# First stage of a graph, attention and expert layer: tiles reordered, third x buffer, S product in plain fp32

## The reference

```
xn  = layernorm(x)
gnn: xt = xn @ weight (4 heads x 64); alpha_l, alpha_r = per-head dot products
     alpha = softmax over heads of leaky_relu(alpha_l[src] + alpha_r[dst])
     out[n] = sum over heads of alpha[n,h] * xt[dst[n], h]      (first 6250 edges only)
mix: qkv = xn @ w_qkv + b; k, v = layernorm per head (8 heads x 32)
     kv = einsum('nd,ne->de', k, v) / 6250 per head;  ret = q @ kv + xn
     out = gelu(ret @ w1 + b1) @ w2 + b2 + xn
x1  = x + gnn + mix
ffn: 8 experts, each relu(bn(. @ W1)), relu(bn(. @ W2)), @ Wo, softmax-weighted by a router
out = x1 + ffn(layernorm(x1))
```

## Time and profile before

| | us |
|---|---|
| median of 3 runs | 1238.53 (1236.17 to 1239.48) |
| the profiled execution | 1239.76 |
| its span, first to last instruction | 1237.8 |
| stage A, first matmul of tile 0 to that of tile 48 | 29.29 to 221.70 |
| between the stages | to 249.29 |
| busy: TensorE / VectorE / ScalarE / GpSimd | 1140.5 / 855.7 / 760.6 / 366.5 |

### The profile page before, as it was taken

One profiled execution on the slowest core, in us unless ns is written; L12 is line 12 of the kernel. 1 busy time (PEld: TensorE's weight loads), 2 busy tenths in 40 slices (PEclk: granted clock), 3 DMA queues, 4 the chain that ended last, 5 costly groups with the idle time before them and its releaser, 6 DMA issues. The chain is left out here.

```text
span 1237.8 us, 19690 instructions
## 1 busy us (share of the span) xinstructions
PE 1140.5 (92%) x6753; PEld 1007.6 (81%) x6753; DVE 855.7 (69%) x1861; ACT 760.6 (61%) x1289; POOL 366.5 (30%) x365
## 2 busy tenths in 40 slices
PE   1878789539999999999999999999999999999998
PEld 1666678438888988988889888888888888888887
DVE  7777678555758677586775967758677586765653
ACT  2667667216666666666666666666666666666665
POOL 2455543460605115051150511505014060220100
PEclk9999899768999999999999999999999999999999
DMA  3343331210001010010100101002010010000000
GB/s 110 104 113 112 95 90 53 74 35 1 19 1 48 6 35 18 1 48 5 36 18 1 48 6 35 19 1 53 1 35 18 5 49 1 21 5 15 4 1 22
DMA packets 60652, 42.16 MB, mean 34 GB/s; under 512 B 26248, under 2 KB 58732, under 8 KB 60552
## 3 DMA queue, kind: packets, MB, share of 16 engines
q1 hardware_dynamic: 56440, 34.28, 10.2%
q0 software_dynamic: 4112, 6.61, 2.2%
HBM read 27.87 MB, written 13.00 MB: 33 GB/s over the span
## 5 line engine op out<-in xcount | busy, mean ns | idle before, releaser
L1097 DVE SCALAR_TENSOR_TENSOR accumulated<-bank,router_w,accumulated 128x256 f32<-128x256 f32 (+1 forms) x392 | 169.9, 478 | 196.7 <-PE bank L220 163.1
L505 ACT ACTIVATE h<-weight_stage 128x512 fp32r<-128x512 f32 (+1 forms) x208 | 114.7, 599 | 209.1 <-PE bank L220 207.0
L218 PE MATMUL bank<-ffn_w_high,h 128*128 128x256 f32 (+1 forms) x784 | 221.8, 283 | 1.0 <-DVE h L901 1.0
L220 PE MATMUL bank<-ffn_w_high,h 128*128 128x256 f32 (+1 forms) x784 | 221.8, 283 | 0.0
L219 PE MATMUL bank<-ffn_w_low,h 128*128 128x256 f32 (+1 forms) x784 | 221.8, 283 | 0.0
L901 DVE TENSOR_TENSOR h_low<-activated,h_high 128x512 fp32r<-128x512 f32 (+1 forms) x208 | 154.6, 756 | 68.0 <-ACT h_high L505 68.0
L601 ACT ACTIVATE weight_stage<-bank,bn_cols 128x512 f32<-128x512 f32 (+1 forms) x208 | 156.8, 754 | 56.8 <-PE bank L220 56.5
L601 ACT ACTIVATE activated<-bank,bn_cols 128x512 f32<-128x512 f32 (+1 forms) x208 | 157.0, 755 | 54.1 <-PE bank L220 52.2
L476 POOL TENSOR_TENSOR residual<-residual,b_rows 128x1024 f32<-128x1024 f32 (+1 forms) x13 | 29.6, 2274 | 522.4 <-DVE residual L1116 522.4
L218 PE MATMUL bank<-xT_high,ffn_w_high 128*128 128x512 f32 (+1 forms) x416 | 163.2, 392 | 0.0
L220 PE MATMUL bank<-xT_high,ffn_w_low 128*128 128x512 f32 (+1 forms) x416 | 159.8, 384 | 0.0
(11 more groups left out here) (188 smaller groups left out, 2234.1 us busy)
## 6 DMA issues: line engine op xcount, KB each, us to landing
x_rows<-in_x SPq DMA_DIRECT2D x24, 512.0 KB, 5.0
node_table<-gathered SPq DMA_DIRECT2D x48, 130.0 KB, 2.0
out<-accumulated SPq DMA_DIRECT2D x12, 512.0 KB, 3.3
weight_stage<-in_L_ffn_W SPq DMA_DIRECT2D x16, 256.0 KB, 4.1
weight_stage<-in_L_ffn_Wo SPq DMA_DIRECT2D x8, 256.0 KB, 2.8
gathered<-node_table,indices POOLq DMA_INDIRECT x49
alpha_l<-node_alpha_l,indices POOLq DMA_INDIRECT x49
accumulated<-in_L_mix_w_qkv SPq DMA_DIRECT2D x1, 768.0 KB
```

What stands on the lines that cost most here:

```text
L218: nc.tensor.matmul(dst, ah, bh, start=(k == 0 and not lead), stop=False)
L220: last = nc.tensor.matmul(dst, al, bh, start=False, stop=(k == n - 1))
L505: return nc.scalar.activation(dst, src, ACT.Copy)
L1097: last = V.scalar_tensor_tensor(a, Yb[b][0:tp, (t % 2) * D:(t % 2 + 1) * D], wts(ch)[0:tp, t, e:e + 1], a, ALU.mult, ALU.add)
```

## The change

- Stage A's loops run over tiles (`TILES`) in place of chunks. Statistics of chunk c+2 are taken in tiles 1 and 2 of chunk c, their square root and reciprocals in tile 3 (chunk 1's in tile 0 at the start). Tile g+4 is normalised in tile g. Transposes, high and low halves of a pair (g+2, g+3) are made in each even tile g.
- A third x buffer: half of `accumulated` (`accx`), so chunk c's rows lie in buffer c mod 3 and chunk c+3 is loaded in chunk c.
- The S product takes the kv rows as they are in plain fp32, one product for each half; the high and low halves of the kv rows are gone, and the normalised kv rows wait for the S product two tiles back. S fills half a bank, so two steps after stage A go.
- The 24 expert weights and `mix_w2` are 25 jobs, job j in tile 1 + 15j/8 rounded down, loaded three tiles ahead into part j mod 3 of `weight_stage`. TensorE and ScalarE wait for all 25 before stage B.
- The scalars are computed straight into `rsA`, `nmA`; GpSimd makes `rs1A` for all at once, and its copies in both stages go.

```diff
+        accx = acc[:, 0, :, :]
+        def x_of(ch):
+            return (xb[:, 0, :, :], xb[:, 1, :, :], accx)[ch.c % 3]
+        def pair_ahead(g):
+            return TILES[g + 2:g + 4] if g % 2 == 0 else []
+        JOBS = [(1, None)] + [(l, e) for e in range(NE) for l in range(3)]
+        JOB_AT = {1 + (j * 15) // 8: j for j in range(len(JOBS))}
 # SyncE
-                    for l, name in enumerate(("L0_ffn_W1", "L0_ffn_W2", "L0_ffn_Wo")):
-                        need(sp, s["wst_lo"], 3 * (e - 1) + l + 1)
...
+            def load_job(j):
+                l, e = JOBS[j]
+                need(sp, s["wst_lo"], j - 2)
...
+            for j in range(2):
+                load_job(j)
+            for T in TILES:
+                g, tp = T.g, T.tp
+                if g + 3 in JOB_AT and JOB_AT[g + 3] >= 2:
+                    load_job(JOB_AT[g + 3])
+                if T.t == 0 and T.ch.c + 3 <= NFULL:
+                    need(sp, s["xnorm"], TPC * (T.ch.c + 1))
+                    load_x(chunk(T.ch.c + 3))
+                need(sp, s["xte"], g + 1)
...
 # GpSimd
+            for T in TILES:
+                g, tp, p = T.g, T.tp, T.g % 2
+                need(pool, s["kvn"], g + 1)
+                need(pool, s["ksum"], g + 1)
+                nc.gpsimd.tensor_tensor(G[0:tp, 0:2 * D], G[0:tp, 0:2 * D], kvn[0:tp, p, :], ALU.add).then_inc(s["ksum"], 1)
+                if g in JOB_AT:
+                    j = JOB_AT[g]
+                    hi, lo = job_parts(j)
+                    need(pool, s["wst_hi"], j + 1)
+                    nc.gpsimd.tensor_tensor(lo, wst[:, j % 3, :], hi.bitcast(fp32), ALU.subtract).then_inc(s["wst_lo"], 1)
 # ScalarE
+            NORM_AT = {0: [], 1: TILES[TPC:TPC + 2]}
+            for T in TILES:
+                if g > 0:
+                    kv_sd(g - 1, 1 - p, P)
+                nc.scalar.activation(sq[0:tp, :], KVb[T.t][0:tp, :], ACT.Square).then_inc(s["sq"], 1)
+                if pair_ahead(g):
+                    t_hi(pair_ahead(g))
+                copy(xte[0:tp, p, :], XTb[p][0:tp, 0:XTW]).then_inc(s["xte"], 1)
+                if T.t == TPC - 1 and T.ch.c + 2 <= NFULL:
+                    x_sd(chunk(T.ch.c + 2))
+                for u in NORM_AT.get(g, TILES[g + TPC:g + TPC + 1]):
+                    xnormed(u)
+                if g in JOB_AT:
+                    copy(hi, wst[:, j % 3, :]).then_inc(s["wst_hi"], 1)
-            kv_hi(NTILES - 1, 0, TAIL)
 # TensorE
-            nc.tensor.matmul(Sb[:, :], onesf[:, :], kvsum, start=True, stop=False, skip_group_check=True)
+            nc.tensor.matmul(Sb[:, 0:2 * P], onesf[:, :], kvsum[:, 0:2 * P], start=True, stop=False, skip_group_check=True)
-                need(pe, s["kvlo"], g + 1)
+                need(pe, s["kvn"], g + 1)
-                    nc.tensor.matmul(dst, kvh[0:tp, p, vc], h2[0:tp, :, p, kc], start=False, stop=False, skip_group_check=True)
-                    last = nc.tensor.matmul(dst[:, 0, :], kvl[0:tp, p, vc], kvh[0:tp, p, kc], start=False, stop=final, skip_group_check=True)
+                    last = nc.tensor.matmul(Sb[:, grp * P:(grp + 1) * P], kvn[0:tp, p, vc], kvn[0:tp, p, kc],
+                                            start=False, stop=final, skip_group_check=True)
 # VectorE
-                need(dve, s["kvhi"], g - 1)
+                need(dve, s["S"], g - 1)
+            for T in TILES:
+                if g > 0:
+                    kv_norm(g - 1, 1 - p, P, (T.t - 1) % TPC)
+                if T.t in (1, 2) and T.ch.c + 2 <= NFULL:
+                    stats_of(chunk(T.ch.c + 2), ((0, 1), (2, 3))[T.t - 1])
+                V.tensor_reduce(ss[0:tp, p, :], ...)
+                if pair_ahead(g):
+                    t_lo(pair_ahead(g))
+                if T.t == TPC - 1 and T.ch.c + 2 <= NFULL:
+                    x_rstd(chunk(T.ch.c + 2))
```

More of the change, by code:

```diff
@@ L225, in wide, with pair_cols @@
             return ap.unsqueeze(len(ap.shape)).broadcast_to(shape)
[L227 to L257, removed]
+        CHUNKS = [chunk(c) for c in range(NFULL + 1)]
+        def pair_cols(pair):
+            u = pair[0].t
+            return slice(u * P, (u + len(pair) - 1) * P + pair[0].tp)
         SETUP_A, SETUP_Q, SETUP_POOL = 42, 2, 12
         LD_SMALL = 27
-        MID_KV, MID_P, MID = 25, 26, 32
+        MID_KV, MID_P, MID = 23, 24, 28
         block = ctx.enter_context(nc.Block())
@@ L268, in _, with load_x @@
         def _(sp):
[L269 to L275, removed]
+            def load_x(ch):
+                sp.dma_start(x_of(ch)[0:ch.tp, 0:ch.nt, :], ch.rows_of(I["x"])).then_inc(s_x[ch.c % 3], 16)
+            load_x(chunk(0))
             sp.dma_start(wqkv, I["L0_mix_w_qkv"].rearrange("(k p) n -> p k n", p=P)).then_inc(s["ld_w"], 16)
@@ L309, in _ @@
             need(sp, s["set_dve"], SETUP_A)
-            def chunk_a(ch, e):
-                if e is not None:
-                    for l, name in enumerate(("L0_ffn_W1", "L0_ffn_W2", "L0_ffn_Wo")):
-                        need(sp, s["wst_lo"], 3 * (e - 1) + l + 1)
[L315 to L327, removed]
-                    sp.dma_start(tab_d[bass.ds(g * P, tp), :], xte[0:tp, t % 2, 0:TAB]).then_inc(s_tab[t % 2], 16)
-                    sp.dma_start(al_d[bass.ds(g * P, tp), :], xte[0:tp, t % 2, TAB:XTW]).then_inc(s_tab[t % 2], 16)
@@ L360, in chunk_b @@
             def chunk_b(ch):
-                if not (isinstance(ch.c, int) and ch.c == 0):
+                if ch.c > 0:
                     store(ch.prev())
-                if not (isinstance(ch.c, int) and ch.c + 2 > NFULL):
-                    loads_b(chunk(ch.c + 2) if isinstance(ch.c, int) else Chunk(ch.c + 2, ch.half + 1, ch.par))
-            phase_b_loop(sp, chunk_b, ahead=2)
+                if ch.c + 2 <= NFULL:
+                    loads_b(chunk(ch.c + 2))
+            for ch in CHUNKS:
+                chunk_b(ch)
             store(LAST)
@@ L881, in chunk_b @@
                         L3(ch, e - 1)
[L882 removed]
+                    elif ch.c > 0:
                         L3(ch.prev(), NE - 1)
```

383 lines of the change are left out of this document (152 added, 231 removed).

## The result

After the change the kernel takes 1188.92 us (median of 4 runs, 1186.54 to 1189.88), beside 1237.35 before on the same chip (4 runs, 1236.09 to 1239.48): a ratio of 0.9603, 95% interval 0.9585 to 0.9621. The profiled execution took 1188.08 us with a span of 1186.2, 51.6 us less span than before. The forecast was 1193, with a stage A 42.0 us shorter.

A forecast was written before the change was run, and what follows sets the result against it. Stage A was taken as held by waits, stage B by a full TensorE. Gains of 42.0 (stage A), 2.1 (its end) and 2.1 (between stages) make 46.2 off 1239.76: 1193.6, called 1193 us, range 1187 to 1199.

The forecast's parts named there:

- the likeliest case: Whole kernel: the forecast of 1193 us with the S product's likely error and the clock's, 1187 to 1199; chance 0.58.
- a margin of 1.1: Stage A: the odd tile's normalising ends at about 6.7 us, the transposes reading it come at 7.8; margin 1.1 us.
- tile 48's end: End of stage A: VectorE's low half goes, GpSimd's sum is late next, and the product over it comes 2.1 us sooner.
- the slower rival: Stage A: short waits keep TensorE at 1.2 GHz, so the gain is lost, up to 1338 us; chance 0.05.
- the rival of a wait at each chunk: Stage A: the 1.2 us wait per chunk stays, twelve make 14 us, so 1207 us; chance 0.17.
- Stage A: 46.4 where 42.0 stood: Stage A: 43.8 us of stalls go and the S product adds 2.3, so tile 48 starts 42.0 us earlier.
- The S product: Stage A: four plain fp32 matmuls take 0.46 us against 0.41 split, +0.05 for each of 46 tiles, 2.3 us.
- The even tile: Stage A: a tile with four transposes takes 3.30 us of unbroken TensorE work, read from tile starts 195.57 and 198.87.
- such bare loads: Stage A: fp32 weight loads standing bare beside each matmul; S product about 0.86 us, stage A 20 us longer.
- The passage: Between the stages: two VectorE steps (0.92 us) and the mix_w2 split (1.19) leave the path, gain 2.1 us.
- The rival's limit of 113 GB/s: Stage A transfers: 129 GB/s needed; if about 113 is the limit, chunks take 14.2 us, +21, 1214; chance 0.10.
- The low half of the kv rows: Stage A, VectorE: four operations a chunk at 0.69 us (0.89 on average) go, leaving 9 of 12.24 us busy.

The follow-up runs named there:

- the two with unread matmuls: Kernel after plus matmuls nobody reads in TensorE's waits: 87 of them, 1180.82 us; 110, with GpSimd's addition moved and index loads ahead of x loads, 1181.39 us.
- the doubled product: Kernel after with each tile's two S products made twice, the second pair into columns that nothing reads: 1206.88 us, ratio 0.9768.
- the doubled table: Kernel after with every tile's table rows written a second time, into a DRAM table that nobody reads: 1190.53 us, ratio 0.9643.
- The split kernel: Kernel after with the S product back in split form, high and low halves of the kv rows on ScalarE and VectorE: 1212.52 us, ratio 0.9816.
- The run with the small sum: Kernel after with the split-form S product, and GpSimd's running sum of each tile cut from 512 to 16 columns: 1195.33 us, ratio 0.9664.
- the kernel with the extra subtraction: Kernel after with one more 128x512 VectorE subtraction for each tile, which nothing reads or waits for: 1206.76 us, ratio 0.9761.
- the kernel with bursts: Kernel after with the weights loaded in bursts again, three loads ahead of each chunk in chunks 0 to 7: 1206.17 us, ratio 0.9763.

## Why the prediction was right, and where its sizes were off

**What held.** The time lies in the likeliest case (1187 to 1199), 4 us under its centre. TensorE's waits that the sum took away are gone from the trace, but for one. The forecast has no wait of the copy on the table's landing; there are seven, 9.3 us, and the one ahead of tile 36 cost TensorE 0.86, against a margin of 1.1 that had left the landing out. The other runs with this stage A (the two with unread matmuls and the one with GpSimd's addition moved) take 140.3 to 140.9 us from tile 1 to tile 48, where the kernel after took 141.4, so this one stall is chance. At tile 48's end the product waits for GpSimd's sum, as said, and 2.07 us were gained where 2.1 stood. Stage B gave 0.3 where 0 stood. The clock stayed full in stage A, so the slower rival had nothing to stand on. The old order's run shows that the rival of a wait at each chunk was the right one to fear: it comes back, at 12.5 us, when statistics, normalising and transposes aren't moved ahead.

**Stage A: 46.4 where 42.0 stood.** Two terms were mis-sized. *The S product* was put at 0.46, +0.05 on the split form; an odd tile went from 2.82 to 2.79, so it is 0.03 below it. That is 0.08 for each of 46 tiles, 3.7 us. The quarter of the row in stage B was right for a stream (0.11 an instruction by the doubled product), but I let the end of the last instruction count, which lies beside the next matmul, though the bound without it, 0.43, stood in the same sentence. *The even tile* was read as 3.30 from 195.57 to 198.87, but the first of these is a matmul behind a wait of 1.14, and the next follows it after 0.34 where it is 0.29 in the tile after (198.87 to 199.16): the cost of a restart. The forecast was 3.35 with the new product, measured 3.23; the product's 0.08 taken off, 0.04 are the restart's, for each of 23: 0.9 us. The rest are 0.3 at tile 1's start and 0.2 in tile 46, which transposes for one short tile only, less the 0.86 of tile 36's stall. Together 4.2 of the 4.4.

The section "LDWEIGHTS" of the Trainium skill's "TensorE: Matmul & The Clock Gate" gives about 107 ns for a load of 128 columns. The trace does not have it on top of the matmuls: four loads and four matmuls take 0.36 together. The prediction's estimate of what such bare loads would add to its stage A, 20 us, is also a little high: 46 times 0.86 less 0.46 is 18.

**The passage: 2.77 where 2.1 stood.** The sum had only what VectorE stopped doing. The products over the sums stand in the passage too, at a clock that had fallen before and not yet after (first the kernel before, then after; the clock is the third figure from the end):

```profile
229.73:231.54 1.81, 1.81 (x8) 1.54 (x7) 0.00 (x0) 0.00 (x0) 0.00 (x0) 0.50 0.46 57
```

```profile
181.22:182.26 1.04, 1.04 (x6) 0.90 (x6) 0.00 (x0) 0.00 (x0) 0.56 (x3) 1.00 1.00 326
```

They take 1.04 where they took 1.81, 0.77 less. The eight fp32 instructions later in the passage took 0.15 more (3.78 for the 3.63 of the earlier trace rows). Together they are the missing 0.67 but for 0.05.

**The transfers.** The rival's limit of 113 GB/s was read off slices that were themselves held by waits. After the change slice 1 moved 153, and the doubled table 166. What a stalled stage moves says nothing of what it could. The copy's 16 waits at 166 show that the landings do take longer there.

**What was right by less than was argued.** The low half of the kv rows was listed as relief for VectorE (0.69, or 0.89 in the mean) and stood in the sum at nothing. Kept, it would have made VectorE's 11.60 us 95% of a chunk of 12.24, and more by its stretch beside GpSimd, a line that the forecast didn't draw. The split kernel's run shows it: 1.03 us each, VectorE at 95%, 26 us. The run with the small sum shows that the stretch is the larger part: VectorE at 93%, TensorE at 99% and 7.5 us. The forecast had the pace right because it dropped the operation, not because it saw that the other two parts hang on it; that much is luck. Each part's removal costs 26, 20 and 12.5 us, 59 in sum, where all three together gave 48; alone, two of them gave 16.6 and 16.1. They share one path: whichever is missing sets the pace. The new order alone in the kernel before was not run, nor the kernel after without the third buffer or without the scalars' new way; that the last two are worth nothing by themselves is argued, not shown.

**Still open.** Whether the doubled table costs 5 us at all (its profiled execution, the fastest of four, is only 0.8 us longer in span than that of the kernel after); and how far the passage could be shortened if GpSimd's additions met no operation of VectorE's.

## What to carry to other kernels

Before a term is taken as free cover, work out what its engine is busy once the waits are gone, with the duration it has beside the other engines' work, not with its shortest. Parts that each lift a limit of one path must be judged together: neither "alone" nor "without" gives their share. A wait taken from one operation in a passage of short steps often reappears at the next; look for what the freed engine will then meet.

## What the runs showed of the hardware

- A subtraction of 128x512 on VectorE with both operands in SBUF took 0.68 us (median) when GpSimd had little to do, and 1.03 in the mean, up to 1.75, beside GpSimd's 128x512 sums. One with an operand in PSUM took 0.68 beside the same sums.
- A VectorE operation of 128x16 was held 2.35 us by a GpSimd addition that began 0.03 us before it; with the addition moved it took 0.18.
- Of plain fp32 instructions of 128 columns at full clock, four took 0.36 us to the start of the next matmul and eight 0.80: 0.11 for each one more.
- TensorE's clock stayed at its full level through all of stage A, also in the kernel with the extra subtraction, where TensorE waited up to 1.4 us at a time (1.00 in its table), and was at 1.2 GHz behind a wait of 2.41 us in the passage. In the kernel with bursts it fell three times right behind a wait of 1.65 us, and not behind two other waits of 1.65.
